# Cross-attention: key and query projections in 13 of a step's 16 slots, value tiles over three steps, and the copies and stacking transfers moved behind them

## The reference, cut to what matters

```python
x = x + L0_attn(layernorm(x), ...)
x = x + L0_xattn(layernorm(x), ctx_768, mask, Wq, Wk, Wv, Wo)   # here
x = x + L0_ffn(layernorm(x), ...)

def L0_xattn(x, context, context_mask, Wq, Wk, Wv, Wo):    # x (8, 512, 512), context (8, 512, 384)
    q = (x @ Wq).reshape(B, N, 16, 32).transpose(0, 2, 1, 3)
    k = (context @ Wk).reshape(B, M, 16, 32).transpose(0, 2, 1, 3)
    v = (context @ Wv).reshape(B, M, 16, 32).transpose(0, 2, 1, 3)
    scores = jnp.einsum('bhid,bhjd->bhij', q, k) * 32 ** -0.5
    scores = jnp.where(context_mask[:, None, None, :], scores, max_neg)
    attn = softmax(scores, axis=-1)
    return einsum('bhij,bhjd->bhid', attn, v).transpose(0, 2, 1, 3).reshape(B, N, 512) @ Wo
```

## Time and profile before

| | |
|---|---|
| median of 3 runs | 3489.23 us (3486.23 to 3492.21) |
| profiled execution | 3487.83 us, span 3486.1 us |
| steps 1 to 28 of cross-attention, slot 2 to slot 2 | 1610.8 to 2313.8 us of the span |
| PE busy over the whole span | 3191.2 us, 92% |

### The profile page before, as it was taken

The page is one execution under the profiler, slowest core; times in us unless marked ns, Lnnn a source line. Parts: engine busy times, 40 slices in busy tenths (PEclk is TensorE's granted clock), DMA queues, the critical chain, the costliest instruction groups (busy, mean ns, idle before and its releaser), DMA issues.

```text
span 3486.1 us, 47184 instructions
## 1 busy us (share of the span) xinstructions
PE 3191.2 (92%) x15056; PEld 2500.3 (72%) x15056; DVE 2590.7 (74%) x4078; ACT 2250.3 (65%) x4127; POOL 1085.2 (31%) x1181
## 2 busy tenths in 40 slices
PE   5999999999999999968999999988989999942998
PEld 4888888888888888855666666655768888731887
DVE  5987878787877777756878788777863469888554
ACT  4876767676767667645777777765432256668665
POOL 1233342423333333334555655556400000001000
PEclk9999999999999999989999999999999999975999
DMA  3443444444344343346666666655722368889764
GB/s 121 171 153 124 131 142 125 131 122 145 121 142 124 131 137 121 103 118 118 118 108 112 124 121 114 123 101 171 232 79 105 112 223 300 313 339 406 272 240 177
DMA packets 273028, 555.49 MB, mean 159 GB/s; under 512 B 28024, under 2 KB 105856, under 8 KB 259472
## 3 DMA queue, kind: packets, MB, share of 16 engines
q1 hardware_dynamic: 268560, 544.08, 52.3%
q10 hardware_dynamic: 4224, 8.39, 0.6%
HBM read 322.72 MB, written 162.30 MB: 139 GB/s over the span
## 4 chain that ended last, share of the span: by engine, by line
PE 37%; DVE 7%; DMA 5%; issue 3%; ACT 1%; SPq 1%; POOL 1%; DVEq 0%; POOLq 0%; ACTq 0%
PE gu_acc L2551 12%; PE ca_mx L2465 3%; PE ca_pj L2445 3%; PE md_acc L2640 3%; PE md_acc L2641 3%; PE md_acc L2642 3%; DVE ca_negm L2036 2%; PE ca_ov L2495 2%; PE ca_ov L2496 2%; PE ca_st L2483 2%; PE ca_pj L2432 2%; DMA ca_q<-ca_ql 1%; PE ca_ms L2455 1%; DVE ca_el L2051 1%; DMA gu_g<-gate 1%
## 5 line engine op out<-in xcount | busy, mean ns | idle before, releaser
L818 POOL TENSOR_SCALAR sa_ex<-sa_ex,sa_rs 128x512 f32<-128x512 f32 x512 | 354.9, 693 | 907.4 <-DVE sa_rs L660 907.4
L655 DVE TENSOR_REDUCE sa_nm<-sa_st 128x1 f32<-128x512 f32 x512 | 350.3, 684 | 223.6 <-PE sa_st L949 219.7
L516 ACT ACTIVATE sa_eh<-sa_tr 128x512 fp32r<-128x512 f32 x512 | 306.2, 598 | 294.5 <-PE sa_tr L959 292.7
L900 PE MATMUL sa_pj<-sa_xh,sa_w 128*128 128x512 f32 x1536 | 455.7, 416 | 3.0 <-DVE sa_xl L633 1.5
L2036 DVE TENSOR_REDUCE ca_negm<-ca_mx 128x2 fp32r<-128x1024 f32 x256 | 312.4, 1220 | 101.6 <-PE ca_mx L2465 98.0
L664 DVE TENSOR_TENSOR sa_el<-sa_tr,sa_eh 128x512 fp32r<-128x512 f32 x512 | 351.2, 686 | 40.7 <-ACT sa_eh L516 33.9
L509 ACT ACTIVATE sa_ex<-sa_st,sa_nm 128x512 f32<-128x512 f32 x512 | 350.8, 685 | 43.6 <-DVE sa_nm L655 39.6
L2328 POOL TENSOR_TENSOR ca_el<-ca_ex,ca_eh 128x512 fp32r<-128x512 f32 x256 | 349.6, 1367 | 64.3 <-ACT ca_eh L1820 64.0
L1812 ACT ACTIVATE ca_ex<-ca_st 128x512 f32<-128x512 f32 x512 | 296.0, 585 | 40.6 <-PE ca_st L2483 39.0
L959 PE MATMUL sa_tr<-top_ident,sa_ex 128*128 128x128 f32 x2048 | 306.9, 272 | 1.8 <-POOL sa_ex L818 1.8
L959 PEld LDWEIGHTS sa_tr<-top_ident,sa_ex 128*128 128x128 f32 x2048 | 254.4, 140 | 71.1 <-POOL sa_ex L818 4.3
(11 more groups left out here) (302 smaller groups left out, 7573.5 us busy)
## 6 DMA issues: line engine op xcount, KB each, us to landing
sa_w<-w_split SPq DMA_DIRECT2D x56, 1536.0 KB, 7.5
gate<-gu_ev SPq DMA_DIRECT2D x24, 1024.0 KB, 4.4
gu_g<-gate SPq DMA_DIRECT2D x48, 512.0 KB, 6.4
gate<-gu_g SPq DMA_DIRECT2D x48, 512.0 KB, 3.8
up<-gu_ev SPq DMA_DIRECT2D x24, 1024.0 KB, 5.7
md_ab<-gate SPq DMA_DIRECT2D x96, 256.0 KB, 6.5
md_ab<-up SPq DMA_DIRECT2D x96, 256.0 KB, 6.9
md_ab<-gate SPq DMA_DIRECT2D x44, 512.0 KB, 11.7
```

Of the source, the lines that this page charges most:

```text
L516: nc.scalar.activation(eh[:, v % ER], tr[:, v % 2], ACT.Copy).then_inc(act_eh, 1)
L655: nc.vector.tensor_reduce(nm[:, u % U:u % U + 1], st[:, u % 2], AX_X, ALU.max, negate=True).then_inc(dve_mx, 1)
L818: nc.gpsimd.tensor_scalar(ex[:, u % U], ex[:, u % U], rs[:, u % U:u % U + 1], 1.0, ALU.mult, ALU.mult).then_inc(pool_n, 1)
L900: yield nc.tensor.matmul(pj[:, bank], w[:, n % 2, m, part, k], xx[:, b % 2, k], start=(i == 0 and k == 0), stop=(i == 2 and k == DK - 1))
```

## The change

The matmuls are the same in number. Keys go from 3, 3, 3 matmuls in slots 0 to 2 to 2, 2, 2, 2, 1 in slots 0 to 4, and queries from 3, 3, 3, 3 in slots 3 to 6 to 2, 1, 2, 1, 2, 1, 2, 1 in slots 5 to 12. One value tile now comes in the step with s % 4 = 2 (slots 12 to 15), two in that with s % 4 = 3, and the fourth in slots 7 to 10 of the batch's own first step. `masked_key`, `high_key` and `low_key` move two slots back. `high_query` moves from slot 7 to 13, `low_query` from 8 to 14, `stack_queries` from 8 to 13, and `load_x` and `load_mask` from slots 7 and 9 to 14 and 15. `stack_keys` stays at slot 8.

```diff
--- before.py
+++ after.py
@@ -1113,7 +1113,7 @@
     OUT_AFTER = FIRST - (OUT_AT - U * N - LA - AV) // OUT_PITCH
     MR = 3 * XD
     STACKS = 16 * 7
-    KPASS, QPASS = (3, 3, 3), (0, 0, 0, 3, 3, 3, 3)
+    KPASS, QPASS = (2, 2, 2, 2, 1), (0, 0, 0, 0, 0, 2, 1, 2, 1, 2, 1, 2, 1)
     VPASS = ((0, 0, 0, 0, 0, 0, 0, 3, 2, 2, 2), (0, 0, 0, 0, 0, 0, 0, 0, 0, 0, 0, 0, 3, 2, 2, 2))
     ORDER = (0, 1, 2, 6, 7, 8, 9, 3, 4, 5)
     HIGH = ("act", "pool", "act", "dve", "act", "pool", "act", "act")
@@ -1386,8 +1386,8 @@
 
         def value_tile(s, i):
 
-            b = s // XG + 1
-            return NT * b + 2 * (s % XG - 2) + i if s % XG >= 2 and b < B else None
+            b, place = (s + 2) // XG, 2 * ((s + 2) % XG) + i - 1
+            return NT * b + place if 0 <= place < NT and b < B else None
 
         def emptied(t):
 
@@ -1711,19 +1711,20 @@
             e.wait_ge(ones_set, 4)
             for G, s, t in slots():
                 n = s + 2
-                if t == 7 and s >= 0 and s % XG == 1 and s // XG + 1 < B:
+                if t == 14 and s >= 0 and s % XG == 1 and s // XG + 1 < B:
                     load_x(s // XG + 1, 0)
                 if t == 5 and 0 <= s < N:
                     max_rows(s)
                 if t == 8 and n < N:
                     stack_keys(n)
+                if t == 13 and n < N:
                     stack_queries(n)
                 if t == 1 and s >= 0 and s % XG == 0 and s // XG + 1 < B:
                     for i in range(NT):
                         load_context(NT * (s // XG + 1) + i)
                 if t % NT == 1 and 0 < s:
                     outputs(s - 1, t // NT)
-                if t == 9 and s >= 0 and s % XG == 1 and s // XG + 1 < B:
+                if t == 15 and s >= 0 and s % XG == 1 and s // XG + 1 < B:
                     load_mask(s // XG + 1)
                     load_x(s // XG + 1, 1)
                 if batch_sums(s, t, 2) is not None:
@@ -1919,9 +1920,9 @@
                     high_exponent(a - 1)
                 if 0 <= a < U * N:
                     exponent(a)
-                if t == 4 and n < N:
+                if t == 6 and n < N:
                     high_key(n)
-                if t == 7 and n < N:
+                if t == 13 and n < N:
                     high_query(n)
                 if batch_sums(s, t, 6) is not None:
                     high_reciprocals(batch_sums(s, t, 6))
@@ -2173,9 +2174,9 @@
                     high_exponent(a - 1)
                 if 0 <= a - 2 < U * N:
                     low_exponent(a - 2)
-                if t == 3 and n < N:
+                if t == 5 and n < N:
                     masked_key(n)
-                if t == 8 and n < N:
+                if t == 14 and n < N:
                     low_query(n)
                 if batch_sums(s, t, 5) is not None:
                     reciprocals(batch_sums(s, t, 5))
@@ -2381,7 +2382,7 @@
                     high_exponent(a - 1)
                 if 0 <= a - 2 < U * N:
                     low_exponent(a - 2)
-                if t == 5 and n < N:
+                if t == 7 and n < N:
                     low_key(n)
                 if out_slot(G) is not None:
                     out_work(out_slot(G))
@@ -2577,7 +2578,7 @@
                 if n < N:
                     if t == 0:
                         work["k"] = key_projection(n)
-                    if t == 3:
+                    if t == 5:
                         work["q"] = query_projection(n)
                     for name, plan, done in (("k", KPASS, pe_k), ("q", QPASS, pe_q)):
                         for _ in range(plan[t] if t < len(plan) else 0):
```

## The result

The changed kernel takes 3563.63 us (3561.09 to 3567.2, three runs), where the kernel before takes 3489.23 us. The ratio is 1.0222, 95% interval 1.0208 to 1.0236: 2.2% slower, 74 us. The forecast was 41 us slower. Its direction was right, its size was not.

The account below looks back on a forecast made before the run. PE was taken to bound cross-attention for some 94%. Step kinds at +2.8, -0.1, +0.7, +2.8 us sum to 46, less waits already there 43, with +2 and -3 42: 3487.8 + 42 = 3530 us, range 3500 to 3566.

Parts of the forecast that it names:

- the stall: Slot 2 of every step: PE waits 2.7 or 2.3 us for the late query stack; 60 to 75 us in all.
- Three transfers: Query stack after `ca_qh`: three transfers of 256 KB take 2.2 + 6.0 = 8.2 us at 131 GB/s.
- an estimated 3.8 us for the three: Query stack by the skill page: 2.0 + 1.8 us, landing before PE comes; the forecast went by the trace instead.
- 14-to-2: Slot 14 to slot 2 of the next step: four stretches sum to 37.1 us, before 28.9; loss 8.2 us a batch.
- 2-to-14: Slots 2 to 14: 17.5, 16.5, 16.5, 18.6 us, sum 69.1, before 71.0; gain 1.9 us a batch.
- the rival on the clock: After slot 2's stalls: TensorE's clock falls each time, 30 x 1.26 = 38 us more, 3568 us; chance 0.08.
- One bound: Lower end of the forecast's own case: no idle left in 2-to-14, 0.3 us less a stack, 5 us at step 29; 3508 us.
- behind them in the queue I take nothing: `load_x` and `load_mask`, about 7 slots later and queued behind the query stacks: cost nothing; 19 us in all if they slow them.
- The stacks are in time: Slot 2: three transfers land within 5.5 us, only smoothing is left, -14 us, 3473 us; chance 0.11.
- Stall and smoothing cancel: Slot 2: the stall is 1 us instead of 2.5, the end within 7 us of now, 3488 us; chance 0.06.

Follow-up runs that it names:

- e1: The kernel before with only the query copies and query stacking moved to slots 13 and 14; 3565.57 us, ratio 1.0218.
- e2: The kernel before with only the value tiles spread over three steps; 3479.84 us, ratio 0.9979.
- e11: The changed kernel with each output store split in two and ten extra matmuls in slot 2 of steps 0 to 27; 3525.77 us, ratio 1.0106.
- e10: The changed kernel with each output store split into two transfers of 32 rows; 3561.72 us, ratio 1.0217.
- e3: The changed kernel with query matmuls done by slot 10, copies in slots 11 and 12, stacking in 11, loads in 12 and 13; 3491.97 us, ratio 1.0014.
- e6: e3 with query matmuls in slots 4 to 8, copies in 9 and 10, stacking in 9, loads in 10 and 11; 3493.56 us, ratio 1.0025.
- e5: e3 without the loads of the queries input for batches 1 to 7; 3473.57 us, ratio 0.9965.
- e9: e6 with each output store split into two transfers of 32 rows; 3461.7 us, ratio 0.9931.

## Why the prediction was wrong in size

*The direction and the stall: right.* The forecast "PE stalls for 2.7 and 2.3 us in slot 2 of every step" met 2.5 us in 28 waits of the loop, 71.1 us in all, inside the 60 to 75 that it named. Three transfers took 7.9 us from the first issue where 8.2 were worked out from the six of the earlier trace rows. DVE's wait for `ca_mx` grew as foreseen, from 82.6 us to 159.7 between 1600 and 2369 us.

The Trainium skill (DMA: Bandwidth & Descriptors, "Anatomy of one DMA") had led to an estimated 3.8 us for the three; the trace does not agree.

*The part that loses.* e1 shows that the late copies and stack alone make the loss, and e2 that the value tiles alone are a gain.

*14-to-2: right, somewhat high.* 35.5 us a batch against 37.1. The largest error is in the first kind, 8.98 against 9.5: its `ca_qh` begins 0.46 us after slot 14, where 0.7 was taken, and the transfers take 7.9 us.

*2-to-14: right as a count, wrong as a time.* The sum had 17.5, 16.5, 16.5 and 18.6 us. In e11, where the clock holds, steps 14 and 15 have 16.51 and 18.55; in the changed kernel steps 12 and 13 have 17.56 and 17.27. So the sum was right to 0.1 us in three kinds. In the second kind 0.8 us more stay. By the distances between starts in step 13, the 16 short matmuls cost 1.6 us where 1.3 were taken, and the one wait, 0.32 us idle on `ca_negm`, costs 0.5 where 0.3 was taken; the other 0.3 us are spread thinly over the stretch.

*The step that failed* is a term that the sum put at nothing: what TensorE's clock loses behind each stall. The reason for leaving it out stands in the rival on the clock: "Against it: step 25's wait of 1.4 us is like the new ones, and the windows of rows 2 hold 1.00 through PE's waits". They are not like them: the longest wait for a stack before is 1.4 us, while the new ones are 2.3 to 3.0 us but for one and come in every step. In the kernel before, seven steps from step 4 on have a wait of 1.24 to 1.27 us on `ca_negm` in 14-to-2, and the clock falls behind one of them (step 8); in the changed kernel it falls behind 19 of 28 stalls. I gave this case 0.08, and it is what happened.

The rival's price came out right, in part by luck. It had one fall of 1.26 us behind each stall, 30 x 1.26 = 38 us. The trace has a fall behind two stalls in three, some of them twice as long, at 36.4 us of full-speed time for the 28, 1.3 us each in the mean. The changed kernel's six batches less those of e11 are 662.05 - 632.02 = 30.0 us, 1.25 us a step, where 28.9 us were lost to the clock; over 30 steps 1.25 us are 38, and the kernel as a whole is 3563.6 - 3525.8 = 38 us slower than e11 (the 4 us of waits on the maxima are in both differences). The forecast without the clock was 3530, and e11 is at 3525.8.

One bound does not come out of its own terms: none of the idle left (0.7 us a batch), 0.3 us less a stack and 5 us at step 29 take 16 us off 3530, which is 3514 and not 3508. Nothing hangs on it.

*The wait on the maxima* was not in the sum at all; I had taken "behind them in the queue I take nothing" for the loads, by SP's order alone. As a wait it is small in the changed kernel (4.3 us), and its removal in e10 gained nothing. It mattered for the variants: it held e3 at 3492 and e6 at 3494.

*The other rivals.* "The stacks are in time" did not occur; it does with the stack at slot 11, in e3, but the 3473 us given for it were not reached there (3492), since M took the stall's place; with the loads left out (e5) the same order takes 3473.6. "Stall and smoothing cancel" did not occur.

*Still open:* why the clock does not fall after every stall. In the batch shown of the changed kernel it falls behind the stalls that open steps 14 and 15 and not behind those of 12 and 13, and with M removed (e10) it falls more often. Nor does the length of the gap decide it alone: in e3, whose waits are 1.9 us at most, the clock falls six times between 1700 and 2250 us. No run here separates what decides it.

## What to carry to other kernels

A stall in a dense matmul loop is to be priced twice: the idle time itself, and half speed for some microseconds behind it (1.25 us a step here, as a mean over stalls of 2.5 us). Before a producer is moved later, add up its transfers at the rate that the trace shows at a full DMA share, and compare that with the time to the consumer. And a small DMA share that stays when everything else is quiet is a sign of transfers that sit on a few engines; giving them an outer dimension of 32, as here, can remove waits that look like another transfer's.

## What the runs showed of the hardware

- The granted clock falls to 0.50 (1.2 GHz) for 3 to 7 us at many, not all, idle gaps of 2.3 to 3.0 us in a loop that is otherwise full (19 of 28 in the changed kernel, 23 of 27 in e10), and at some gaps below 2 us (one of seven of 1.25 us in the kernel before, and in e3). Ten matmuls in each gap, thrown away, made the kernel 36 us faster (e10 to e11).
- Three transfers of 256 KB from SBUF to SBUF fill all 16 DMA engines (share 1.02 to 1.11) at only 123 to 133 GB/s, while the load of `ca_xq` moves 408 GB/s at the same share (1.06, e6).
- Stores of 64 rows of 2 KB with an outer dimension of 2 run on two of 16 engines (share 0.13 at 51 GB/s) and leave them a backlog: in e6 a transfer of 8 KB, issued at the end of a 2 MB load, held PE until 8.2 us after its issue, and with the stores spread over more engines (e9) PE does not wait for it.
